# New order of the pieces of a step in an fp32 attention, and an unrolled second expert mixture

## The reference, cut to what matters

```python
# L0 cross attention: 16 heads of 64, queries 256 per batch, keys and values 4092 per batch
q_in = x @ Wq + lora(x);  k_in = ctx @ Wk + lora(ctx);  v_in = ctx @ Wv + lora(ctx)
s = einsum('bhid,bhjd->bhij', q, k) * SCALE
o = einsum('bhij,bhjd->bhid', softmax(s), v)
# L1 mixture: 8 experts (2 chosen per token) and one shared, hidden width 512, 512 tokens
h = silu(x @ gate_e) * (x @ up_e);  out += weight_e * (h @ down_e)
```

## Time and profile before

| | before |
|---|---|
| runs | 2288.22 us median (2287.87 to 2291.06), 3 runs |
| profiled execution | 2282.97 us, its span 2281.3 us |
| mean granted TensorE clock | 0.941 |
| PE / DVE / ACT / POOL busy | 87% / 43% / 44% / 29% |
| first attention, loop over the steps | from 158.7 to about 1240 us of the span |
| second mixture, its PE work | from 2114.3 to 2276.9 us |

### The profile page before, as it was taken

One profiled execution on the slowest core, in us unless ns is written; L12 is line 12 of the kernel. 1 busy time (PEld: TensorE's weight loads), 2 busy tenths in 40 slices (PEclk: granted clock), 3 DMA queues, 4 the chain that ended last, 5 costly groups with the idle time before them and its releaser, 6 DMA issues. The chain is left out here.

```text
span 2281.3 us, 33850 instructions
## 1 busy us (share of the span) xinstructions
PE 1993.0 (87%) x13572; PEld 1343.7 (59%) x13572; DVE 990.1 (43%) x1525; ACT 1004.0 (44%) x1353; POOL 667.8 (29%) x316
## 2 busy tenths in 40 slices
PE   6688999999989999999999776849898899687999
PEld 2465666656656566665666544438445744465787
DVE  3365455465564655546553244237002600365222
ACT  1143444444444444444442232116897699232221
POOL 1004445454444545546555212010000000100321
PEclk9798999999999999999999888779898999898999
DMA  5130000000200000000002100013453454200121
GB/s 183 54 104 5 1 15 5 6 15 6 66 24 5 15 1 15 6 15 5 1 1 73 56 1 1 1 49 84 81 90 72 84 84 84 75 1 1 56 83 65
DMA packets 89856, 90.51 MB, mean 40 GB/s; under 512 B 29896, under 2 KB 79760, under 8 KB 86384
## 3 DMA queue, kind: packets, MB, share of 16 engines
q1 hardware_dynamic: 86848, 85.97, 15.6%
q10 hardware_dynamic: 2864, 2.51, 0.4%
HBM read 58.57 MB, written 8.91 MB: 30 GB/s over the span
## 5 line engine op out<-in xcount | busy, mean ns | idle before, releaser
L739 POOL TENSOR_TENSOR sums<-sums,probs 128x1024 f32<-128x1024 f32 x224 | 532.6, 2378 | 454.6 <-ACT probs L772 395.6
L824 DVE TENSOR_REDUCE part_max<-psum_banks 128x2 f32<-128x1024 f32 (+1 forms) x256 | 312.9, 1225 | 125.8 <-PE psum_banks L983 121.9
L772 ACT ACTIVATE probs<-psum_banks 128x1024 f32<-128x1024 f32 x240 | 245.7, 1024 | 169.7 <-PE psum_banks L1023 157.7
L817 DVE TENSOR_TENSOR keys<-psum_banks,keys 64x512 fp32r<-64x512 f32 x256 | 176.2, 688 | 303.4 <-ACT keys L750 298.7
L1037 PE MATMUL psum_banks<-probs,values 128*64 128x256 f32 x2048 | 281.7, 397 | 0.2 <-ACT probs L775 0.2
L750 ACT ACTIVATE keys<-psum_banks 64x512 fp32r<-64x512 f32 x256 | 151.5, 592 | 292.8 <-PE psum_banks L956 289.6
L2406 ACT ACTIVATE probs<-psum_banks,k_inv_norm 128x1024 f32<-128x1024 f32 x256 | 257.9, 1207 | 2.5 <-PE psum_banks L2421 2.4
L1037 PEld LDWEIGHTS psum_banks<-probs,values 128*64 128x64 f32 x2048 | 125.2, 137 | 100.1 <-issue 60.2
L1009 PE MATMUL psum_banks<-q_hi,keys 128*128 128x256 f32 x1024 | 180.9, 300 | 0.0
L1009 PEld LDWEIGHTS psum_banks<-q_hi,keys 128*128 128x128 f32 x1024 | 140.7, 192 | 53.9 <-issue 52.6
L2433 PE MATMUL psum_banks<-probs,values 128*32 128x256 f32 x2048 | 166.3, 398 | 2.3 <-ACT probs L2406 2.3
(11 more groups left out here) (428 smaller groups left out, 3016.9 us busy)
## 6 DMA issues: line engine op xcount, KB each, us to landing
k_pairs<-keys SPq DMA_DIRECT2D x192, 128.0 KB, 4.2
ctx_tok<-in_ctx SPq DMA_DIRECT2D x16, 384.0 KB, 3.4
wk_pair<-wkv_parts SPq DMA_DIRECT2D x16, 256.0 KB, 2.9
wv_quad<-wkv_parts SPq DMA_DIRECT2D x8, 512.0 KB, 3.7
w_gate_up<-in_L_ffn_gate_proj_w SPq DMA_DIRECT2D x8, 512.0 KB, 4.1
w_gate_up<-in_L_ffn_up_proj_w SPq DMA_DIRECT2D x8, 512.0 KB, 5.0
w_down<-in_L_ffn_down_proj_w SPq DMA_DIRECT2D x8, 512.0 KB, 5.9
ctx_tok_b<-in_ctx SPq DMA_DIRECT2D x8, 384.0 KB, 4.5
```

The costliest lines, as they stand in the source:

```text
L739: pool.tensor_tensor(sums[:, :, :, :], probs[:, 0, :, :, :] if step == 1 else sums[:, :, :, :], probs[:, step % SLOTS, :, :, :], ALU.add). ...
L772: act.activation(probs[:, step % SLOTS, :, :, :], scores, ACT.Exp, scale=SCALE0).then_inc(p_ready, 1)
L817: dve.tensor_tensor(keys[rows(1 - h), m % 2, h, columns_of(c)], psum[rows(h), bank, :], keys[rows(h), m % 2, h, columns_of(c)].bitcast(F32 ...
L824: dve.tensor_reduce(part_max[:, :, i, c], psum[:, bank:bank + 2, 0:width], AX, ALU.max).then_inc(m_read, 1)
```

## The change

First attention:
- The loop starts at step -1 (was -4); the spread of unit 0's maxima and the first keys piece of unit 1 stand before it. Unit 1's keys pieces come one every second step, its maxima one a step (the last two in one step).
- Of later units, each maximum comes one step later, the spread at step 14 of a unit (was 13).
- PE's order in a step: begin scores, *first* pieces (values and turn_a), output part, shift, *second* pieces (keys), spread, low queries, max pieces unless the step is odd or 14, weigh, max pieces of odd steps and 14, *behind* pieces (values, turn_b), denominators.
- Both values pieces of two steps stand in the odd step, one first, one behind.
- The spread uses 64-column tiles, two heads at a time, and the shift is one DVE instruction.
- Query splits are made by halves at steps 3, 5 (high) and 7, 9 (low), instead of all at step 9.

Second mixture: one unrolled stream over 36 tiles; down weights and hidden values are split too, and the down product is three fp32r passes; all low parts are DVE's, POOL has no work; the down product of a tile follows the gate and up product of the next one also across experts; an expert's fetch waits for the splits of the expert in its slot alone.

```diff
-FIRST_STEP = -4
+FIRST_STEP = -1
-    return (m - 1) * STEPS + 2 * c - 4 if m > 1 else EARLY_KEYS[c]
+    return (m - 1) * STEPS + 2 * c - 4 if m > 1 else 2 * c - 2
-    return (m - 1) * STEPS + 2 * c + i - 3 if m > 1 else EARLY_MAX[2 * c + i]
+    return (m - 1) * STEPS + 2 * c + i - 2 if m > 1 else min(2 * c + i - 1, 13)
-    return m * STEPS - 3
+    return m * STEPS - 2
+def is_late(g):
+    return g % 2 == 1 or g % STEPS == STEPS - 2
...
-        for step in range(STEPS):
-            behind[(2 * quad - 1) * STEPS + step].append(("values", quad, step))
+        for step in range(0, STEPS, 2):
+            first[(2 * quad - 1) * STEPS + step + 1].append(("values", quad, step))
+            behind[(2 * quad - 1) * STEPS + step + 1].append(("values", quad, step + 1))
...
+                spread_maxima(0)
+                prepare(("keys", 1, 0))
                 for g in range(FIRST_STEP, LAST_STEP):
                     if ahead is not None:
                         begin_scores(ahead // STEPS, ahead % STEPS)
-                    for m in range(UNITS):
-                        if g == spread_step(m):
-                            spread_maxima(m)
-                    for piece in front[g]:
+                    for piece in first[g]:
                         prepare(piece)
                     if g >= LAST_STEP - STEPS:
                         output_part(g % STEPS)
                     if ahead is not None:
+                        shift_scores(ahead // STEPS, ahead % STEPS)
+                    for piece in second[g]:
+                        prepare(piece)
+                    for m in range(1, UNITS):
+                        if g == spread_step(m):
+                            spread_maxima(m)
+                    if ahead is not None:
                         finish_scores(ahead // STEPS, ahead % STEPS)
-                    for piece in top[g]:
-                        prepare(piece)
+                    if not is_late(g):
+                        for piece in top[g]:
+                            prepare(piece)
                     if g >= 0:
                         weigh(g // STEPS, g % STEPS)
+                    if is_late(g):
+                        for piece in top[g]:
+                            prepare(piece)
+                    for piece in behind[g]:
+                        prepare(piece)
                     if g >= 0 and g % STEPS == STEPS - 1:
                         denominators(g // STEPS)
-                    for piece in behind[g]:
-                        prepare(piece)
...
+                for i in range(TILES):
+                    gate_up(i)
+                    if i >= 1:
+                        down(i - 1)
+                down(TILES - 1)
...
-                            last = pe.matmul(psum[:, 4 + t, 0:D], hidden[:, m, t * P:(t + 1) * P], wd[:, slot, m, :],
-                                             start=m == 0, stop=m == MT - 1)
+                        for k, (h, w) in enumerate(((hidden_hi, wd_hi), (hidden_hi, wd_lo), (hidden_lo, wd_hi))):
+                            last = pe.matmul(psum[:, 4 + t, 0:D], h[:, m, t * P:(t + 1) * P], w[:, e % 2, m, :],
+                                             start=m == 0 and k == 0, stop=m == MT - 1 and k == 2)
...
+                    act.activation(hidden_hi[:, m, :], hidden[:, i % 2, :], ACT.Copy).then_inc(hidden_hi_ready, 1)
+                    if m >= 1 and e + 1 < EXPERTS:
+                        split(e + 1, m - 1)
...
+                    dve.tensor_tensor(hidden_lo[:, m, :], hidden[:, i % 2, :], hidden_hi[:, m, :].bitcast(F32),
+                                      ALU.subtract).then_inc(hidden_lo_ready, 1)
+                    if m >= 1 and e + 1 < EXPERTS:
+                        split(e + 1, m - 1)
+                    if m == 0 and e >= 1:
+                        add(e - 1)
```

More of the change, by code:

```diff
@@ L602, in l0_attention @@
     Q_SLOTS = 3
-    front, top, behind = steps_of_pieces()
-    in_bank0 = [p for g in range(FIRST_STEP, LAST_STEP) for p in front[g] + behind[g]]
+    first, second, top, behind = steps_of_pieces()
+    in_bank0 = [("keys", 1, 0)] + [p for g in range(FIRST_STEP, LAST_STEP) for p in first[g] + second[g] + behind[g]]
     before_in_bank0 = dict(zip(in_bank0, [("keys", 0, CHUNKS - 2)] + in_bank0))
@@ L901, in _ @@
                 maxima(0)
-                high_queries(1)
+                shifts(0)
+                prepare(("keys", 1, 0))
                 for g in range(FIRST_STEP, LAST_STEP):
-                    for piece in front[g]:
+                    for piece in first[g]:
                         prepare(piece)
-                    for m in range(UNITS):
+                    for m in range(1, UNITS):
                         if g == spread_step(m):
                             shifts(m)
-                    for piece in top[g]:
+                    for piece in second[g] + top[g]:
                         prepare(piece)
@@ L1010, in begin_scores, with shift_scores @@
                                       q_hi[:, m % Q_SLOTS, h, :], start=j == 0, stop=False)
+                def shift_scores(m, step):
+                    bank = 4 + 2 * (step % 2)
+                    if step == 0:
+                        pe.wait_ge(shift_ready, m + 1)
+                    for h in range(2):
+                        pe.matmul(psum[:, bank + h, :], ones_r[rows(h), :],
+                                  shift[rows(h), m % 2, None, :].to_broadcast([HD0, 2, L]), start=False, stop=False)
                 def finish_scores(m, step):
@@ L1938, in _, with product @@
-                with pe.Fori(0, EX // 2) as i:
-                    for slot in range(2):
-                        expert(i * 2 + slot, slot, i)
-                expert(EX, 0, EX // 2)
+                def product(i, bank, which):
+                    e, m = i // MT, i % MT
+                    cols = slice(m * P, (m + 1) * P)
+                    passes = [(w, x, c) for w, x in ((w_hi, x_hi), (w_lo, x_hi), (w_hi, x_lo)) for c in range(DC)]
+                    for k, (w, x, c) in enumerate(passes):
+                        last = pe.matmul(psum[:, bank, :], w[:, e % 2, which, c, cols], x[:, c, :],
+                                         start=k == 0, stop=k == len(passes) - 1)
+                    return last
@@ L1950, in expert, with split @@
[L1950 to L1959 removed]
+                def split(e, part):
+                    raw, hi, _ = weight_part(e, part)
+                    if part == 0:
+                        act.wait_ge(arrived[e % 2], (e // 2 + 1) * 48)
+                    if e >= 2:
+                        act.wait_ge(down_done, (e - 1) * TT)
+                    act.activation(hi, raw, ACT.Copy).then_inc(w_hi_ready, 1)
@@ L1994, in _ @@
[L1994 to L2014 removed]
+                for part in range(3):
+                    split(0, part)
```

243 lines of the change are left out of this document (113 added, 130 removed).

## The result

The changed kernel takes 2230.68 us (median of four runs, 2228.37 to 2233.24); the kernel before, timed beside it, 2288.05. The ratio is 0.975 (95% interval 0.973 to 0.977): 57 us less, where 82 were forecast. The time lies inside the forecast range, but 25 us above its centre, where rival (a) stood with 2231: the range held because it was wide enough for that rival.

A forecast was written before the change was run, and what follows sets the result against it. TensorE (PE), plus its waits, was taken to bound the attention. Attention -72 and second mixture -12.5 from the profiled 2282.97 give 2198.5, 2203.7 in terms of the runs, 2206 with 2 us for the values' margin; range 2190 to 2240.

The forecast's parts named there:

- rival (a): Attention: changes of tile shape cost double at some 250 places with unseen neighbours (+25 us), total 2231; chance 0.14.
- Price list: Microseconds: H high-scores 0.66, S shift 0.33, L low-scores 0.24, M maximum 0.33, K keys 1.26, V values 1.28, W weighing 1.01.
- H S K L M W: PE's order in an even attention step without values: 0.66 + 0.43 + 1.26 + 0.24 + 0.33 + 1.01 = 3.93 us.
- Extras of a stretch: Attention: query splits fall in DVE's holes; the spread of maxima takes some 0.6 us for 1.09, without its 1.02 wait.
- First stretch: First 16 steps of the attention: keys and maxima dealt out step by step, 59.1 us against 76.48, -17.
- Last stretch: Last stretch of the attention, without new keys: gains nothing.
- Values' margin: Attention steps with values: product at 2.16 us after keys' end, split ready at 2.14 or 2.19; 2 us set aside.
- Mixture: Second mixture: split down product 1.42 us per tile for 1.73, saving 11.2; last tile +0.8, start -2.1; sum -12.5.
- Rival (c): Second mixture: weight loads bound the down product, 2.3 us a tile against 1.73, +20 instead of -11; total 2237, chance 0.04.
- (b): First stretch of the attention keeps its low clock or its waits: +12 to 17 us, total 2221; chance 0.1.
- (d): Attention: the values piece in front holds the scores, keys split 1.1 us later; -72 becomes +38, total 2314; chance 0.03.
- (e): Only the mixture gains, since new waits in the attention equal the old: total 2276; chance 0.05.

## Why the prediction was right, and what failed in it

- *PE bounds the loop, its waits are what can go.* Right: PE busy went from 95% to all of a value stretch.
- *Price list.* H, S, M, V, W and the late maximum came out within 0.05. **The step that failed is the sum of the even step, H S K L M W,** where I gave S its change of shape towards K but took K at 1.26 and L at 0.24, their prices among other neighbours. The 1.26 was read between H and S, with a change on one side only, and the 0.24 between S and M, with none; by the count that I used for H (0.66 with two tenths in it) K was due another tenth, and so was L. Measured: K 1.37 and L 0.34. In each of 119 keys pieces that is 0.2, so 24 us, the largest part of the 29 by which the attention fell short. Putting K back behind H gave 22, of which 19 by the shapes (it takes away two whole changes, with the tenths of H and S that the forecast did count) and 3 by the clock of the first stretch. The rest of the shortfall is in the lines below; together they are more than 29, since the stretches before were 5 us longer in sum than the two that the forecast multiplied. Rival (a), double price at neighbours not seen before, had the time, 2231, and was right at two of its three, S before K and K before L; at the third, W before M, the late maxima cost just what I had for them.
- *Extras of a stretch.* Right in kind: the burst of query splits was worth 6 us, the spread went from 1.09 with a wait of 1.0 to 0.58 without.
- *First stretch,* forecast 59, measured 64.8 with the keys piece ahead of the loop: the waits at steps 12 and 13 were in the sum, not the low clock behind them; my sum took every piece at its full-clock price. Against kernels that had the same wait and kept the clock, the low clock cost 1.4 us in step 12 (9.09 for 7.71) and 1.5 in step 14 (6.41 for 4.92).
- *Last stretch,* forecast no change, measured 57.1 for 54.6: it got one values piece more (1.28) and six of the dearer keys steps.
- *Values' margin,* two hundredths: the odd step took 5.28 for 5.23, 2 us in all as I had set aside.
- *Mixture,* forecast 12.5. The mixture from its first product on gave 9 (tile 4.18 for 4.15, tail as forecast), its start 2.3 (PE begins 2.5 us after the first high part, 2070.9 to 2073.4, where it began 4.8 after it, 2109.5 to 2114.3): 11.5 in the traces, 15 (11 to 18) in the medians. Rival (c), by the rule on weight loads in the Trainium skill, TensorE: Matmul & The Clock Gate, The mechanism, falls: twelve matmuls with a load each take 1.43, 0.119 each, though a load alone is recorded with 0.19.
- *Rivals (b), (d), (e).* (b) came true for a third of its size. (d) did not: the odd step with values took 0.05 more than forecast, not 1.1. (e) did not: the attention alone got 43 us shorter. The chances for the outcome do not fit those of the rivals, either: (e), within 2% of before, had 0.05, but "same" only 0.02.

## What to carry to other kernels

Where TensorE has no waits left, its time depends on which pieces stand side by side: write the order of a step as a row of shapes and count the changes, each at its price from the trace, on both of its sides. Put a piece behind another for cover only if the wait that it covers is longer than the changes of shape that it makes; here full-array pieces grouped together (H K, V H) and 64-row pieces together (S L M) were worth some 19 us, and a rule for all steps cost 8 us where half of them had no wait to hide.

## What the runs showed of the hardware that was not expected

- A change between 64 rows and the full array costs about 0.2 us in either direction, half on each side of it. S K L cost 0.43 + 1.37 + 0.34 = 2.14, and K S L 1.25 + 0.34 + 0.23 = 1.82, for the same matmuls, and H before them 0.66 and 0.58. The profile counts PE as busy all the while; only the rows of the weight loads show it.
- The same wait of PE was followed by a fall of the clock in some traces and not in others. Behind 1.3 us in step 13, step 14 has a granted clock of 0.73 and takes 6.4 us in the changed kernel, and 1.00 and 4.9 without late maxima; with keys before the shift it takes 4.5 at 1.00. Behind 2.1 us in step 12 that step has 0.81 in the changed kernel, and 1.00 with the query splits at one step and with keys before the shift. Waits of 1.1 us in later bare stretches (query splits at one step) were followed by steps of 4.1 as always. What makes the difference stays open, and with it some 3 us in a comparison of any two of these kernels.
- Time before the attention and between it and the mixture moved by some microseconds from run to run (827 to 831 us between them, 824 in one), with nothing changed in them. It is as large as the smaller effects here, so those were read from the attention's own length.
